# DLRM tower on one core: the products inside pairs of fields laid on all four quarters of the TensorE array

## What is computed

```python
e = jnp.stack([tbl_0[ids[:, 0]], ..., tbl_39[ids[:, 39]]], axis=1)   # 512 x 40 x 64
vi = x[:, i_idx, :]                       # i < j, 780 pairs
vj = x[:, j_idx, :]
viW = jnp.einsum('bpd,pde->bpe', vi, W)   # W: 780 x 64 x 64
out = jnp.einsum('bpe,bpe->bp', viW, vj)
...
h = jnp.concatenate([z, dense_ctx], axis=1)
h = jnp.maximum(h @ W_top1 + b_top1, 0.0)
h = jnp.maximum(h @ W_top2 + b_top2, 0.0)
y = h @ W_top3
```

## Time and profile before

| | |
|---|---|
| median of 3 runs | 380.26 us (380.23 to 380.48) |
| the profiled execution's own time | 379.78 us |
| its span, first to last instruction | 378.0 us |
| mean granted TensorE clock | 0.982 |
| TensorE busy | 348.8 us (92%) |
| VectorE busy | 277.1 us (73%) |
| inner units (L498) | 40 records, 9.7 us |

### The profile page before, as it was taken

One profiled execution on the slowest core, in us unless ns is written; L12 is line 12 of the kernel. 1 busy time (PEld: TensorE's weight loads), 2 busy tenths in 40 slices (PEclk: granted clock), 3 DMA queues, 4 the chain that ended last, 5 costly groups with the idle time before them and its releaser, 6 DMA issues.

```text
span 378.0 us, 4628 instructions
## 1 busy us (share of the span) xinstructions
PE 348.8 (92%) x1784; PEld 125.0 (33%) x1784; DVE 277.1 (73%) x287; ACT 45.4 (12%) x73; POOL 171.0 (45%) x261
## 2 busy tenths in 40 slices
PE   0864886899999999999999999999999999999997
PEld 0532332433333333333333333333333333333342
DVE  3999998569687777866758877796778788878420
ACT  2112310111010030101010120000000000300142
POOL 6888888506788775544535553252344100000000
PEclk9978898999999999999999999999999999999999
DMA  5355632012162421121122112220221000000000
GB/s 186 90 167 163 180 125 62 14 57 69 30 264 76 134 74 28 58 69 33 46 71 69 45 37 66 69 69 10 65 68 59 10 2 0 2 1 0 2 0 0
DMA packets 11448, 24.29 MB, mean 64 GB/s; under 512 B 3857, under 2 KB 3857, under 8 KB 11298
## 3 DMA queue, kind: packets, MB, share of 16 engines
q1 hardware_dynamic: 7330, 19.79, 15.6%
q0 software_dynamic: 4096, 4.20, 5.4%
HBM read 23.98 MB, written 0.00 MB: 63 GB/s over the span
## 4 chain that ended last, share of the span: by engine, by line
PE 86%; DVE 9%; DMA 2%; ACT 1%; issue 1%; SPq 0%
PE y_ps L491 46%; PE z_ps L515 24%; DVE one_hot L392 7%; PE t_ps L470 4%; PE y_ps L523 3%; PE t_ps L446 3%; PE t_ps L461 2%; DMA table<-in_small_tables 2%; PE y_ps L498 2%; PE y_ps L553 2%; DVE x L401 1%; DVE table_parts L386 1%; DVE prod L422 1%; PE t_ps L559 0%; ACT x L326 0%
## 5 line engine op out<-in xcount | busy, mean ns | idle before, releaser
L422 DVE TENSOR_TENSOR prod<-y_ps,x 128x1024 f32<-128x1024 f32 x190 | 220.8, 1218 | 61.6 <-PE y_ps L491 58.6
L491 PE MATMUL y_ps<-x,w_sb 64*128 64x512 f32 x760 | 185.5, 617 | 12.1 <-DVE prod L422 5.1
L302 POOL DMA_INDIRECT rows<-in_tbl,ids_sb x128 | 126.0, 984 | 124.0 <-PE y_ps L491 92.7
L491 PEld LDWEIGHTS y_ps<-x,w_sb 64*128 64x128 f32 x760 | 67.1, 188 | 117.2 <-issue 59.1
L515 PE MATMUL z_ps<-prod,selector 128*32 128x512 f32 x780 | 94.3, 598 | 0.0
L297 POOL MEMSET spacer<- 128x256 f32 x127 | 44.3, 349 | 0.2
L515 PEld LDWEIGHTS z_ps<-prod,selector 128*32 128x32 f32 x780 | 20.4, 109 | 67.0 <-issue 36.3
L392 DVE TENSOR_SCALAR one_hot<-ids_all,numbers 128x512 fp32r<-128x512 int32 x64 | 34.4, 607 | 0.0
L446 PE MATMUL t_ps<-one_hot,table_parts 128*128 128x512 f32 x56 | 18.6, 479 | 14.0 <-DVE one_hot L392 9.7
L328 ACT ACTIVATE x<-t_ps 128x512 f32<-128x512 f32 x15 | 9.0, 599 | 156.4 <-PE t_ps L461 151.4
L446 PEld LDWEIGHTS t_ps<-one_hot,table_parts 128*128 128x128 f32 x56 | 11.9, 226 | 21.6 <-issue 12.7
(11 more groups left out here) (36 smaller groups left out, 59.8 us busy)
## 6 DMA issues: line engine op xcount, KB each, us to landing
w_sb<-in_w_units SPq DMA_DIRECT2D x25, 512.0 KB
ids_all<-in_ids_one_hot SPq DMA_DIRECT2D x8, 256.0 KB
table<-in_small_tables SPq DMA_DIRECT2D x8, 256.0 KB
rows<-in_tbl,ids_sb POOLq DMA_INDIRECT x128
w_sb<-in_w SPq DMA_DIRECT2D x1, 1792.0 KB
w_sb<-in_w SPq DMA_DIRECT2D x1, 512.0 KB
ids_sb<-in_ids SPq DMA_DIRECT2D x1, 80.0 KB, 2.0
z_sb<-in_dense_t SPq DMA_DIRECT2D x1, 32.0 KB
```

The source lines that it names most:

```text
L302: pool.indirect_dma_start(rows[:, n % ROW_SLOTS, bt, h * D:(h + 1) * D], None, tables[f], bass.IndirectOffsetOnAxis(ap=ids_sb[:, bt, f:f + ...
L422: dve.tensor_tensor(prod[:, at:at + 2, :], y_ps[:, s % Y_SLOTS], leaf, ALU.mult).then_inc(prod_ready, 1)
L491: ins = pe.matmul(y_ps[:, slot, h, :], w_sb[own, c % W_SLOTS, at:at + P], x[own, m, :], start=True, stop=True)
```

## The change

In an inner unit, `n` (0 to 3) numbers the pairs of fields. Before, a matmul of it reads low partitions and writes high ones, or reads high and writes low. In program order: low rows to high columns into bank 0, the same quarter into bank 1, then high rows to low columns into bank 0, and the same quarter into bank 1. After it, bank 0 gets low to low and high to high, and bank 1 gets low to high and high to low, in this order. Each of the four matmuls has another quarter. To fit, `x_mix` is filled otherwise: two of the four copies of a unit now cross from one half of the partitions to the other. The host lays out the weights and the rows of `W_top1` by `pairs_of`; their sizes are the same.

```diff
@@ pairs_of
-    return [(1 - n % 2, n // 2, n % 2, 2 * (a + n) + 1 - n % 2, 2 * (a + n) + n % 2) for n in range(4)]
+    return [(n % 2, n // 2, n % 2 ^ n // 2, 2 * (a + n) + n % 2, 2 * (a + n) + 1 - n % 2) for n in range(4)]
@@ mix (ScalarE)
                 for n in range(4):
-                    k, own = 4 * q + n, slice(D * (n % 2), D * (n % 2) + D)
+
+                    k, into, other = 4 * q + n, D * (n % 2 ^ n // 2), D * (1 - n % 2)
                     wait_x(act, k)
-                    act.activation(x_mix[own, q % MIX_SLOTS, n // 2, :], x[own, k, :],
+                    act.activation(x_mix[into:into + D, q % MIX_SLOTS, n // 2, :], x[other:other + D, k, :],
                                    ACT.Copy).then_inc(mixed, 1)
@@ multiply (TensorE)
-                for own, into, first in ((low, high, 1), (high, low, 0)):
-                    for bank in range(2):
-                        k = 4 * unit[1] + 2 * bank + first
-                        ins = pe.matmul(y_ps[into, slot, bank, :],
-                                        w_sb[own, c % W_SLOTS, at + D * bank:at + D * bank + D], x[own, k, :],
-                                        start=True, stop=True)
+                for bank in range(2):
+                    for h, own in enumerate((low, high)):
+                        ins = pe.matmul(y_ps[(low, high)[h ^ bank], slot, bank, :],
+                                        w_sb[own, c % W_SLOTS, at + D * bank:at + D * bank + D],
+                                        x[own, 4 * unit[1] + 2 * bank + h, :], start=True, stop=True)
                 ins.then_inc(y_ready, 1)
```

## The result

The changed kernel takes 375.68 us, the median of 6 runs (375.08 to 377.03), against 380.31 us for the 6 runs of the kernel before beside it (380.23 to 380.80). The ratio is 0.9883, 95% interval 0.9863 to 0.9904. The forecast was 376.85 us with a range of 376.2 to 378.3: the direction is right, but the time is 1.2 us under the forecast and 0.5 us under the range. It is also under 375.9 us, the lowest sum that the prediction had.

The account below looks back on a forecast made before the run. TensorE, gapless from 94.3 to 354.5 us, was taken as the bound. Four later inner units saving 0.86 us each, the first 0, gave 379.78 - 3.4 = 376.4 us profiled, median 376.85 us, range 376.2 to 378.3.

Parts of the forecast that it names:

- What bounds the kernel: TensorE has no gap from 94.3 to 354.5 us, so what it saves there comes off the end.
- Matmuls: 1.01 us a unit, 0.86 saved: Inner unit's four matmuls all run at once: two steps of 0.43 us plus 0.15 entry, instead of 1.87 us.
- the bound of serial loads: If an inner unit's first four weight loads came one behind another, it would save only 0.60 us.
- Second to fifth unit, nothing given back: The four later inner units each save 0.86 us of TensorE and nothing else becomes late: 3.4 us.
- First inner unit: saving 0: At 50.05 us the chain runs through VectorE, whose product comes only at 58.58, so a shorter unit saves nothing.
- Copies at no cost: ScalarE's copies into `x_mix`, 627 ns each, cost 0 on the path, even if crossing ones took twice as long.
- The rule on PSUM banks: Trainium skill: different row tiles cannot access one PSUM bank simultaneously; as a wait, inner units would stay at 1.87 us, 380.3 us.
- The sum: Profiled execution 379.78 - 3.4 = 376.4 us, 0.5 us under the median of 380.26, which goes to 376.85 us.
- Two at a time: Inner units still run only two matmuls at once, as before; 380.3 us, chance 0.07.
- something given back: Serial loads with another slot wait, or a lower clock, return part of the saving; 378.5 us for the clock, chance 0.05.
- slower: Quarters sharing rows or a bank run one by one, an inner unit takes 3.6 us; 387.1 us, chance 0.04.
- Rival 2: Part given back by serial loads or by TensorE's clock dropping behind the first inner unit; 1.7 us, 378.5 us, chance 0.05.

Follow-up runs that it names:

- third_before: The kernel before, unchanged, run once more on a further chip; mean 380.5 us, ratio 1.0007 to the kernel before beside it.
- hold_more: Changed kernel with two waits: gathers from the 19th wait for the sixth group of comparisons, from the 25th for the last; 373.57 us, ratio 0.9803.
- hold_before: Kernel before with one wait: gather 24 (counted from 0) and later ones start once the last one-hot matrix is made; 377.70 us, ratio 0.9874.

## Why the prediction was right and wrong

- **What bounds the kernel.** Right: TensorE without a gap from 94.3 us on, and each saving there comes off the end (295.3 to 291.9 us).
- **Matmuls: 1.01 us a unit, 0.86 saved.** Right: 1.02 and 0.85. Eight loads lie within 0.21 us; the bound of serial loads (0.60 us saved) was not needed.
- **Second to fifth unit, nothing given back.** Right, with the slack forecast. At the fifth unit the next cross unit had 0.5 us of room, and TensorE did not wait for it.
- **First inner unit: saving 0.** Supported, not settled: 0.9993 and 0.9985, both intervals reaching 1. The product behind it did not stand at 58.58, as the prediction had it, but came at 57.62, as the seventh group was shorter.
- **Copies at no cost.** Right: 629 ns.
- **The rule on PSUM banks.** It has no effect on this form: 1.02 us with shared banks and with separate ones.
- **The sum.** Its term for the change holds, 3.4 us. What failed is the step from the profiled execution to the median, "That one lies 0.5 us under the median of 380.26, which goes to 376.85 us". It took the start-up of the trace before as fixed, 82.7 us to the turn of pair 7, and the range was made from the price of a matmul alone. The runs put in its place a start-up that varies: the whole time by up to 4 us in the kernel before and 3 us in the changed one. It is made of 1.0 to 1.5 us for each group of comparisons that gathers do or don't slow, and of the granted clock behind the last group, 22.5 to 25.2 us to the turn of pair 7. Between the two first traces the clock was the same, 0.93. Their 1.1 us are the seventh group, 1.22 us shorter, less 0.46 us for the eighth, and 0.3 us of smaller shifts. The trace before held the sign: its third group took 3.25 us beside a gather of 4.23, and the others 4.25 to 4.60. I read that line as a mean of 607 ns a comparison and didn't look at its two values. With half of those 4 us on either side, an estimate made afterwards, the range would have been about 375 to 379 us.
- **Rivals.** Two at a time, something given back, and slower: none occurred. Rival 2 had the clock behind the first inner unit in it, as a cost of the change. The runs show it vary in that stretch without the change (25.2 us in `third_before` against 24.1). No rival was about a start-up that varies by itself, which is where the miss was.

On the first chip this looked like a real 1.2 us more, since the six runs of the kernel before lay within 0.6 us. It took the second chip to show the kernel before spread over 4 us.

## To carry to other kernels

When matmuls are 64 x 64, count the quarters of the array that are in use, not the matmuls: four on four quarters take little more than one. Before comparing two kernels whose difference is a microsecond, cut both traces at an event behind the noisy part and compare the rest: 3.4 us was exact in every trace, and the whole time never was. And look for an engine's instructions of one size that have two durations: here one wait on GpSimd, for gathers that are not urgent, was worth about as much as the change (ratio 0.9874 against 0.9883), and both together 0.981. The two free groups explain 2.2 to 2.7 us of its 4.4 us (3.25 each for 4.24 to 4.60); the rest is not explained.

## What the runs showed of the hardware that I had not expected

- Four float32 matmuls of 64 x 64 x 512 on four quarters take 1.02 us, entry included; on two quarters 1.86 to 1.87 us. In either case the two orders tried make no difference.
- Comparisons of 128 x 512 on VectorE and gathers issued by GpSimd have two ways to share: 475 ns each with one gather held for 3.7 to 4.2 us, or 501 to 825 ns each (in the seventh group of `before`) with most gathers at 0.95 us. In the versions without a wait, each group of eight took either 3.25 us or 4.2 to 4.7. The 3.66 us of the fifth group in `hold_more` are of neither kind: there the wait stopped GpSimd at 33.4 us, in the middle of the group. What decides is open. In every free group that met a gather, the gather started within 0.4 us of the group's first comparison, but one started within 0.1 us of the eighth group in `after` too, and that group took 4.71 us.
- With the same work and the same idle time, TensorE took 22.5, 24.1 or 25.2 us for one stretch, at granted clocks of 1.00, 0.93 and 0.86. The length of its wait at the start of the stretch (2.6, 3.9 and 3.9 us, but 1.8 us in `hold_before` at 0.93) doesn't order these.
